# A fused gated-attention and ternary-FFN kernel: opening loads reordered, four row normalisations moved from GpSimd to VectorE, the written-out order replaced

## The reference, cut to what matters

```python
z1 = layernorm(x)                                  # rows of 1024
q = softmax_over_head_dim(Wq @ z1);  k = softmax_over_columns(Wk @ ctx);  v = Wv @ ctx
out = Wo @ (per head: (k @ v.T).T @ q) + bo
x = x + tanh(g_xattn) * out / norm(out) * g * sqrt(128)
z2 = layernorm(x)
scale = mean(abs(w));  wq = round(clip(w / (scale + eps), -1, 1)) * scale     # w_gate, w_up, w_down
x = x + tanh(g_ffn) * ((z2 @ gate.T) * (z2 @ up.T)) @ down.T
```

## Time and profile before

| | us |
|---|---|
| median of 3 runs (1431.26 to 1431.88) | 1431.77 |
| the profiled execution | 1432.09 |
| its span, first to last instruction | 1430.1 |
| PE busy | 1352.4 (95%) |
| DVE busy | 924.7 (65%) |
| ACT busy | 643.0 (45%) |
| POOL busy | 460.8 (32%) |
| mean granted TensorE clock | 0.975 |

### The profile page before, as it was taken

How to read it: one execution, slowest core, us unless ns; L and a number is a source line. 1 busy time by engine, 2 the same in 40 slices (tenths; PEclk the granted TensorE clock), 3 DMA queues, 4 the chain that set the end, 5 groups by cost and what they waited for, 6 DMA issues and landing times.

```text
span 1430.1 us, 23953 instructions
## 1 busy us (share of the span) xinstructions
PE 1352.4 (95%) x9612; PEld 961.6 (67%) x9612; DVE 924.7 (65%) x1385; ACT 643.0 (45%) x973; POOL 460.8 (32%) x281
## 2 busy tenths in 40 slices
PE   4577689999999999999999999999999999999999
PEld 2344377855788658775688648775688648875884
DVE  5878778788768767766576756856576756521220
ACT  4778878854435333443344334443344343320220
POOL 1169936654222432322312322322323313110000
PEclk9778889999999999999999999999999999999999
DMA  9948999958545473347325753447325643211001
GB/s 350 408 149 225 282 340 296 227 137 172 110 90 99 107 156 72 94 87 163 89 54 110 141 129 72 105 84 165 89 46 118 136 99 77 60 45 60 1 1 44
DMA packets 328431, 189.06 MB, mean 132 GB/s; under 512 B 295873, under 2 KB 296001, under 8 KB 328321
## 3 DMA queue, kind: packets, MB, share of 16 engines
q1 hardware_dynamic: 321408, 162.37, 46.8%
q10 hardware_dynamic: 6912, 25.17, 5.8%
HBM read 97.32 MB, written 16.78 MB: 80 GB/s over the span
## 4 chain that ended last, share of the span: by engine, by line
PE 80%; POOL 7%; issue 4%; DMA 4%; DVE 2%; SPq 2%; ACT 1%; POOLq 0%; ACTq 0%; DVEq 0%
PE ps L889 37%; PE ps L914 21%; PE ps L702 7%; PE ps L703 7%; PE ps L704 7%; POOL w_dn L1452 1%; PE ps L857 1%; POOL inter_buf L1452 1%; DMA inter_buf<-in_gate_w 1%; POOL stage_c L1452 1%; SPq L649 1%; PE ps L865 1%; DMA qs<-in_wo 1%; DMA eT<-p 1%; POOL qs L1480 1%
## 5 line engine op out<-in xcount | busy, mean ns | idle before, releaser
L889 PE MATMUL ps<-zT,w_gu 128*128 128x256 f16 x5504 | 624.0, 273 | 3.7 <-DVE zT L1129 3.2
L889 PEld LDWEIGHTS ps<-zT,w_gu 128*128 128x128 fp8e4 x5504 | 539.4, 98 | 80.2 <-DVE zT L1129 3.6
L914 PE MATMUL ps<-w_dn,inter_buf 128*128 128x512 fp8e4 x1376 | 307.4, 379 | 1.0 <-ACT inter_buf L926 0.7
L914 PEld LDWEIGHTS ps<-w_dn,inter_buf 128*128 128x128 f16 x1376 | 134.5, 99 | 157.4 <-ACT inter_buf L926 1.1
L1480 POOL TENSOR_TENSOR qs<-qs,q_stat 128x1024 f32<-128x1024 f32 x64 | 123.8, 1938 | 312.7 <-DVE q_stat L1356 312.2
L926 ACT ACTIVATE gate<-ps 128x256 f32<-128x256 f32 (+1 forms) x176 | 66.8, 379 | 285.7 <-PE ps L889 285.0
L1407 DVE SCALAR_TENSOR_TENSOR gate<-ps,gate 128x256 f32<-128x256 f32 (+1 forms) x176 | 73.8, 420 | 153.5 <-ACT gate L926 152.8
L1129 DVE TENSOR_TENSOR inter_buf<-gate,inter_buf 128x256 f16<-128x256 f32 (+1 forms) x176 | 93.6, 532 | 64.6 <-ACT inter_buf L926 64.3
L926 ACT ACTIVATE inter_buf<-gate 128x256 f16<-128x256 f32 (+1 forms) x176 | 73.0, 415 | 101.3 <-DVE gate L1407 101.2
L1026 ACT ACTIVATE ek<-ps,kbias,k_unit 128x1024 f32<-128x1024 f32 x64 | 76.8, 1200 | 67.8 <-DVE kbias L1273 60.4
L1065 ACT ACTIVATE qs<-qs,l_used 128x1024 f32<-128x1024 f32 x64 | 73.2, 1144 | 75.1 <-DVE qs L1348 70.2
(11 more groups left out here) (152 smaller groups left out, 1974.8 us busy)
## 6 DMA issues: line engine op xcount, KB each, us to landing
xb<-in_x ACTq DMA_DIRECT2D x16, 512.0 KB, 4.8
x_dram<-xb SPq DMA_DIRECT2D x16, 512.0 KB, 3.0
fin<-x_dram SPq DMA_DIRECT2D x32, 256.0 KB, 3.9
out<-fin SPq DMA_DIRECT2D x32, 256.0 KB, 2.0
cx_raw<-in_ctxn ACTq DMA_DIRECT2D x15, 512.0 KB, 4.2
q_raw<-in_x ACTq DMA_DIRECT2D x15, 512.0 KB, 4.7
...
```

The costliest lines, as they stand in the source:

```text
L889: last = nc.tensor.matmul(ps[:, j % 2, s * T:s * T + T], w_gu[:, w, k, :], zT[:, h, k, :], start=(k == 0 and h == 0), stop=(k == NC - 1 an ...
L914: mm = nc.tensor.matmul(ps[:, hf, :], lhs, w_dn[:, j, hf * 512:hf * 512 + 512], start=(u == 0), stop=(u == total - 1))
```

## The change

It does four things.

1. `consts` issues Wv and Wo right after the context of batch 0, then x, then Wq. The transposed context of batch 0 (`ld_ctxT`) waits on ACT for Wv and Wo to have landed, and stands behind `l_hi(0)`. The two `xb` loads of batches 0 and 1 move from the head of ACT's list to due 25.8 and 61.2 us, and each waits for `kt` of its own batch.
2. `q32` and `z` of batches 0 and 1 run on DVE instead of POOL, as the same instruction (`tensor_scalar`, 128x1024, float32).
3. All tables of due times are replaced. The small FFN steps `gcopy`, `gmul`, `i_hi`, `i_lo`, `reload`, `finish` and `st_out`, until now at fixed distances behind their `gu` or `down` step, and the weight loads, until now due when their slot came free, have due times of their own (`FFN_PLAN`, `LOAD_AT`).
4. The staging slots are a written list `SLOT` in place of the function `stage_slots`. It differs in the 34 places from number 90 to 123, all of them chunks of w_down.

The same 84 PE steps stand ahead of the first `gu` in the old and in the new order, the same 454 ahead of the first `gu` of group 3, and the last 525 of PE's 961 steps stand in the same order. Some due times, in us:

| step | due before | due after |
|---|---|---|
| `prod` | 7.6 | 5.7 |
| `lmax(2)` / `cscale(0)` on DVE | 9.3 / 10.6 | 10.0 / 7.0 |
| `c_hi(0)` | 11.2 | 7.5 |
| `kt(0,0)` / `qt(0,0)` | 13.8 / 22.8 | 24.0 / 17.9 |
| `kt(1,0)`, ahead of `ctxk(0,1)` only after | 64.3 | 59.5 |
| `wpart` of gate, `wscale` of gate | 73.7, 75.6 | 73.6, 74.6 |
| `kmax(1,0)` | 74.1 | 70.7 |
| first and last `wquant` of gate and up | 76.3, 163.6 | 75.4, 158.5 |
| `x2a(1,1)`, `z(1)`, `zt(1)` | 153.8, 159.1, 163.8 | 157.2, 162.3, 163.2 |
| first `gu` | 169.2 | 168.8 |
| `gu(0,2,0)` | 180.4 | 179.0 |
| first `down` | 275.2 | 283.7 |
| first `gu` of groups 1, 2, 3, 7 | 339.7, 509.6, 669.9, 1286.1 | 345.8, 506.3, 674.3, 1290.6 |

```diff
-FFN_FROM = (1692, 3397, 5096, 6699, 8305, 9911, 11517, 12861)
+FFN_FROM = (1688, 3458, 5063, 6743, 8349, 9955, 11561, 12906)
...
@@ consts (SyncE)
                 sp.dma_start(ek[:, 0, HD:N], wk).then_inc(s_wk, 16)
                 sp.dma_start(cx_raw[:, :], ctx_rows[rows_of(0), :]).then_inc(ctx_in, 16)
-                sp.dma_start(ek[:, 0, 0:HD], wq).then_inc(s_wq, 16)
-                sp.dma_start(q_raw[:, :], x_rows[rows_of(0), :]).then_inc(xq_in, 16)
                 sp.dma_start(ek[0:DH, 1, :], wv).then_inc(s_wvo, 16)
                 sp.dma_start(qs[0:DH, 0, :, :].rearrange("p a b -> p (a b)"), wo).then_inc(s_wvo, 16)
+                sp.dma_start(q_raw[:, :], x_rows[rows_of(0), :]).then_inc(xq_in, 16)
+                sp.dma_start(ek[:, 0, 0:HD], wq).then_inc(s_wq, 16)
...
@@ ld_xr, ld_ctxT (ScalarE)
                 wait(act, x2_stored, 16 * (i - 1))
-                if i < GB + BY_PE:
+                if i < GB:
+                    act.wait_ge(kt_ready, PAIRS * i + 1)
+                elif i < GB + BY_PE:
                     wait(act, zt_ready, i - 1)
...
                 wait(act, ct_lo_s, i)
+                if i == 0:
+                    act.wait_ge(s_wvo, 32)
...
@@ VectorE
+            def q32_(i, _):
+                if i >= ON_DVE:
+                    return
+                wait(dve, rstd1, i + 1)
+                nc.vector.tensor_scalar(q_raw[:, :], q_raw[:, :], mv[:, 0:1], mv[:, 3:4], ALU.subtract,
+                                        ALU.mult).then_inc(q32, 1)
+
+            def z(i, _):
+                if i >= ON_DVE:
+                    return
+                wait(dve, rstd2, i + 1)
+                wait(dve, x2_ready, 2 * i + 2)
+                nc.vector.tensor_scalar(z32, xb[:, i % 2, :], mv2[:, 0:1], mv2[:, 3:4], ALU.subtract,
+                                        ALU.mult).then_inc(z_ready, 1)
...
@@ GpSimd, in q32_ and in z
+                if i < ON_DVE:
+                    return
```

More of the change, by code:

```diff
@@ L47 @@
 BY_PE = 2
+ON_DVE = 2
 DOWN_PARTS = 6
-FFN_FROM = (1692, 3397, 5096, 6699, 8305, 9911, 11517, 12861)
+FFN_FROM = (1688, 3458, 5063, 6743, 8349, 9955, 11561, 12906)
 PLAN = {
[L56 to L71, removed]
[6 rows of a table removed]
-    "kmax": [[199, 226, 374, 428], [741, 773, 796, 841], [1267, 1305, 1353, 1485], [1510, 2040, 2059, 2134],
[4 rows of a table removed]
-    "kexp": [[215, 249, 406, 454], [757, 799, 823, 949], [1286, 1336, 1382, 1512], [1556, 2057, 2089, 2377],
[4 rows of a table removed]
-    "ktr": [[241, 432, 518, 567], [770, 920, 998, 1041], [], [], [], [], [], [], [], [], [], [], [], [], [],
@@ new lines @@
+    "ld_ctx": [[], [209], [518], [1115], [1486], [2236], [3103], [3870], [4685], [5672], [6476], [7270], [8092],
+        [8876], [9698], [10482]],
+    "cabs": [[48], [326], [868], [1244], [1739], [2323], [3173], [3908], [4733], [5732], [6527], [7338], [8167],
+        [8944], [9773], [10550]],
+    "csum": [[65], [428], [899], [1422], [2170], [3036], [3789], [4624], [5616], [6412], [7224], [8044], [8830],
+        [9650], [10436], [11256]],
+    "cscale": [[70], [444], [904], [1433], [2193], [3052], [3816], [4648], [5638], [6417], [7233], [8049],
+        [8839], [9655], [10445], [11261]],
@@ new lines @@
+    "c_hi": [[75], [458], [1081], [1452], [2208], [3058], [3822], [4654], [5644], [6430], [7239], [8064],
+        [8845], [9670], [10451], [11276]],
+    "c_lo": [[190], [488], [1099], [1467], [2221], [3088], [3855], [4670], [5657], [6452], [7255], [8077],
+        [8861], [9683], [10467], [11289]],
+    "ld_ctxT": [[57], [447], [], [], [], [], [], [], [], [], [], [], [], [], [], []],
+    "ct_hi": [[116], [640], [], [], [], [], [], [], [], [], [], [], [], [], [], []],
+    "ct_lo": [[431], [672], [], [], [], [], [], [], [], [], [], [], [], [], [], []],
@@ new lines @@
+    "ctxk": [[470, 608], [860, 1125], [1542, 1842], [2299, 2534], [2934, 3137], [3685, 3891], [4323, 4532],
+        [5337, 5525], [5989, 6189], [6830, 7048], [7617, 7824], [8436, 8654], [9223, 9430], [10042, 10260],
+        [10829, 11036], [11635, 11831]],
+    "krec": [[581], [880], [1609], [2205], [2872], [3633], [4262], [5290], [5950], [6777], [7550], [8383],
+        [9156], [9989], [10762], [11573]],
+    "cc_hi": [[651], [1162], [1883], [2566], [3167], [3923], [4562], [5555], [6225], [7085], [7855], [8691],
+        [9461], [10297], [11067], [11861]],
@@ new lines @@
+    "rstd2": [[1166], [1610], [2693], [3290], [3853], [4540], [5479], [6166], [6910], [7696], [8516], [9302],
+        [10122], [10908], [11683], [12455]],
+    "z": [[1175], [1623], [2722], [3317], [3860], [4548], [5487], [6174], [6917], [7704], [8523], [9310],
+        [10129], [10916], [11691], [12463]],
+    "zt": [[1184], [1632], [], [], [], [], [], [], [], [], [], [], [], [], [], []],
+    "zt_hi": [[1201], [1653], [], [], [], [], [], [], [], [], [], [], [], [], [], []],
+    "zt_lo": [[1218], [1674], [], [], [], [], [], [], [], [], [], [], [], [], [], []],
@@ L299, in ffn_times @@
         at.append((start + t, "gu", (g, j, s)))
-        if s == 1 or j == IC:
-            at += [(start + t + dt, kind, (g, j))
-                   for kind, dt in (("gcopy", 20), ("gmul", 24), ("i_hi", 29), ("i_lo", 33))]
     for n, t in enumerate(down):
         at.append((start + t, "down", (g, n // DOWN_PARTS, n % DOWN_PARTS)))
-    for k in range(4):
-        first, done = start + down[k * DOWN_PARTS], start + down[k * DOWN_PARTS + DOWN_PARTS - 1] + 17
-        back = first - 25 if k > 1 else start + gu[-20] if g else max(SIGN_AT) + 15 + k
-        at += [(back, "reload", (g, k)), (done + 4, "finish", (g, k)), (done + 14, "st_out", (g, k))]
+    for kind in FFN_PLAN:
+        at += [(start + t, kind, (g, n)) for n, t in enumerate(FFN_PLAN[kind][g])]
     return at
```

237 lines of the change are left out of this document (112 added, 125 removed), and 230 rows, old and new, of tables (DOWN_AT, FFN_PLAN, GU_AT, LOAD_AT).

## The result

Over 20 runs each, the changed kernel takes 1436.05 us (1431.56 to 1442.59), the kernel before 1431.19 us (1428.14 to 1433.19). The ratio is 1.0038, 95% interval 1.0027 to 1.0049: slower by 5.4 us by the ratio (the two medians lie 4.9 us apart). The profiled execution of the changed kernel took 1437.52 us, its span is 1435.4 us against 1430.1.

What follows compares the result with a forecast made beforehand. It took the end as set by the time of the first gu, with PE nearly always busy after it. Terms of -3.1, -2.0 and +1.8 against 1432.09, less 0.3 for the median, gave 1428.5 us, range 1423 to 1435.5.

Steps and rivals of the forecast that it cites:

- Part 1: Opening loads reordered: Wo lands earlier, fewer sums remain behind the last weight chunk; -3.1 us, bounds 0 and -5.9.
- Rival C: Opening: ACT held at the second xb load until kt(1,0), first rounding 3.7 us later; end 1435.3 us, chance 0.16.
- Part 2: Before the first gu: four operations moved from POOL to DVE, 1.2 us each there; -2.0 us, bounds 0 and -5.
- Part 3: Behind the first gu: new places of small FFN steps delay groups 1 and 3; +1.8 us, bounds -3 and +6.
- From group 3 on: 0: From group 3 to the end: PE's order hardly differs, so no time gained or lost, 0 us.
- the -3.3 of the sum: Whole kernel: -3.1 - 2.0 + 1.8 = -3.3 us against the profiled execution's 1432.09 us.
- E: Opening: POOL and DVE block each other, three moved operations cost 3.0 us in all; end 1431.5 us, chance 0.06.

Runs made afterwards that it cites:

- old_loads_new: Kernel before with its own tables and only the opening loads of the change: 1427.91 us, ratio 0.9972 to the kernel before.
- norm_on_pool: Changed kernel with the four norms (q32 and z of batches 0 and 1) back on POOL: 1443.05 us, ratio 1.0082 to the kernel before.
- xr5_later: Changed kernel with only ld_xr(5), the load of x for batch 5, due 355.3 instead of 347.3 us: 1428.88 us, ratio 0.9981 to before.
- after_again: Changed kernel timed once more with nothing edited: 1437.49 us, ratio 1.004 to the kernel before.

## Why the prediction was wrong

**Up to the first `gu`** Parts 1 and 2 summed to -5.1 us. Measured: -1.6 in the profile, -2.8 as the mean of the seven profiles with this opening, which is what the new loads do alone (-2.9). One reading ahead of them was off as well, without weight in the sum: the sixth slice of PE stands at 8, so it is from the seventh on that PE is busy nine tenths.

**Part 1, loads: right.** Forecast -3.1 us at the first rounding, measured -4.0 in the profile after, -2.8 in old_loads_new (81.92), and -4.0 us of time for the loads alone. ACT's last sum ended at 78.7 for a forecast of 79.1. `c_hi(0)` started at 12.7 for a forecast of 13. The DMA share stayed at 1.02 and 1.03 up to 75 us. Rival C's place was read rightly and its condition didn't come about: `kt(1,0)` started at 64.97, not 74.7. One link is weaker than I took it: in the seven profiles the first rounding lies between 79.6 and 82.3 us, and the two latest go with the two earliest first `gu` (179.98, 180.07).

**Part 2, norms to DVE: the value isn't a number of its own.** The forecast was -2.0. The term counted what `z(1)` does to POOL and to its own path (2.6 us, borne out by the 3.0 of norm_on_pool), and set DVE's side at 3.6 us of load. It left out `z(0)`, which in the old order takes 2.6 us beside a busy POOL and delays what is behind it, and whose turn `z(1)` takes on DVE: `qsub(2,0)`'s, and so the PSUM banks. Within the new order the move is worth -6.0 us, within the old +2.9. Seen from the first `gu`, the moved norms and the new order of the opening together came to nothing: the changed opening gives 181.6 as a mean of seven profiles, the new loads alone 181.4 in one. The operation took 0.805 us on DVE, between the 1.2 I took and the 0.6 estimated from the Trainium skill (VectorE: DVE Perf Modes, section "Mode 2×_2P"); `z(0)`, beside a busy POOL, took 1.55. The row is `q32(1)`, from DVE by line, 80 to 184 us, shapes kept apart:

```profile
L1427 DVE TENSOR_SCALAR q_raw<-q_raw,mv 128x1024 f32<-128x1024 f32 x1 | 0.8, 805 | 0.0
```

**Part 3 is the step that failed.** I set the stretch behind the first `gu` at +1.8 with bounds of -3 and +6, from due times and from the 4.2 us of idle there. Measured: +5.7 to group 3's first `gu`. Worked out again from the runs, the new order of groups 1 and 2 is 2.0 us better than the old one (330.9 against 332.9, xr5_later), and the stall costs 7.8. My bounds came from sums over due times, which hold only the waits that their maker knew of; I didn't lay the transfers of the new table beside each other. The table shows it: `turn_q(4,2)` due at 345.0, `turn_k(5,0)` at 348.5 and `reload(1,0)` at 343.5 stand around `ld_xr(5)` at 347.3. The trace of before even had such a case in it, which I hadn't read: a `turn_k(2,3)` that held SP's queue for 11.37 us from 181.82 on, beside two 512 KB loads on ACT's queue and weight loads on SP's.

```profile
181.82 11.37 SPq L649 DMA_TRANSPOSE kT<-k  x1
```

What the term left out is this one stall, 7.8 us; with it the stretch is +5.7 for a forecast of +1.8, without it -2.0. Why a load and two transposes that meet a second load take so much longer stays open.

**"From group 3 on: 0" failed by 1.2 us.** I looked at PE's order there, which hardly differs, and not at ACT's and DVE's. The swap of `z(15)` and `i_lo(6,20)` made a wait of 1.4 us where there had been 0.2.

**Luck.** With the stall out, xr5_later stands 2.7 us under before (ratio 0.9981), near the -3.3 of the sum. That is no support for the sum: the opening gave -2.8 for -5.1, the stretch behind it -2.0 for +1.8, the rest +1.2 for 0, and the errors cancel.

**Rivals.** None named the mechanism. E (POOL and DVE in each other's way, 3.0 us) named an event that is there: `z(0)` took 1.55 us in the changed kernel and 2.63 in the old order, for 0.81 where nothing held it. The longest hold was on an instruction that E didn't name, `c_lo(2,0)` (5.08 for the usual 1.28); it came with a first `gu` 1.2 to 2.8 us later, and what it cost isn't shown. The Trainium skill (SBUF — State Buffer, section "Who interferes with whom") speaks of one blocking the other for a whole instruction; here a DVE instruction with two inputs was held across four of POOL's, until POOL paused, and in after_again it got its turn between two of them.

**The account of the whole change**, from the ratios: loads -4.0, the stall in group 1 +8.4, the swap near group 6's first `down` +1.9; that makes +6.3 of a measured +5.4, and the rest, -0.9, is all that 3500 new due times and four moved operations come to once those two places are out. Each of these pieces is a difference of ratios with an interval of 2 us or so either way, and the loads were priced in the old order, so the rest can't be told from 0. Putting the two places right gives 1427.9 (ratio 0.9968), and the new loads alone 1427.9 (0.9972): the larger edit buys nothing over the smaller one that can be measured.
